# Weight preparation, skip rows, short expert turns and 21 added gathers moved in one graph and expert layer kernel

## The reference, cut to what matters

```python
xn = layernorm(x)
# 1. graph attention over 100000 edges (src, dst), 4 heads of 64
feat = (xn @ W).reshape(N, 4, 64)
ex   = exp(leaky_relu(el[src] + er[dst]) - emax[dst])
rst  = segment_sum(feat[src] * ex, dst) / segment_sum(ex, dst)
gnn  = xn + elu(rst + bias)
# 2. linear attention over all rows, 8 heads, feature map elu + 1
kv = k^T v (per head);  mix = (q kv / (q sum k)) @ wo + bo
x  = x + gnn + mix
# 3. eight experts, top two of each row
xn2 = layernorm(x);  probs = softmax(xn2 @ Wr + br);  top 2 of 8
y_e = gelu((xn2 * ln_g[e] + ln_b[e]) @ W1[e] + b1[e]) @ W2[e] + b2[e]   # 256 -> 1024 -> 256
out = x + sum over the two chosen experts of weight * y_e
```

## Time and profile before

| | |
|---|---|
| time, median of 3 runs | 1894.84 us (1893.95 to 1897.71) |
| profiled execution: its time | 1891.82 us |
| its span, first to last instruction | 1890.1 us |
| mean granted TensorE clock | 0.937 |
| PE busy | 1581.7 us (84%) |
| DVE busy | 1368.5 us (72%) |
| POOL busy | 1218.3 us (64%) |
| ACT busy | 1079.1 us (57%) |

### The profile page before, as it was taken

The page is one execution under the profiler, slowest core; times in us unless marked ns, Lnnn a source line. Parts: engine busy times, 40 slices in busy tenths (PEclk is TensorE's granted clock), DMA queues, the critical chain, the costliest instruction groups (busy, mean ns, idle before and its releaser), DMA issues. The chain is left out here.

```text
span 1890.1 us, 46784 instructions
## 1 busy us (share of the span) xinstructions
PE 1581.7 (84%) x11358; PEld 1300.0 (69%) x11358; DVE 1368.5 (72%) x3833; ACT 1079.1 (57%) x3043; POOL 1218.3 (64%) x1135
## 2 busy tenths in 40 slices
PE   7858777788787989888887778629999999999995
PEld 5635555455566777777775666517888889888884
DVE  6656567677667888888888999897666656665662
ACT  4655566566666666677666776563444444444441
POOL 2077777777777777777677776105666666666663
PEclk8978899999999999999998888658999999999998
DMA  7745565566544555555555665652333333333332
GB/s 223 247 122 138 168 174 164 165 176 179 150 117 127 155 150 150 141 152 145 142 139 179 183 202 162 200 199 45 53 48 53 49 48 50 53 50 49 46 53 24
DMA packets 149158, 239.37 MB, mean 127 GB/s; under 512 B 27536, under 2 KB 114824, under 8 KB 147624
## 3 DMA queue, kind: packets, MB, share of 16 engines
q0 software_dynamic: 61216, 132.39, 30.4%
q1 hardware_dynamic: 85944, 103.15, 16.8%
q10 hardware_dynamic: 1744, 0.85, 0.2%
HBM read 180.78 MB, written 55.52 MB: 125 GB/s over the span
## 5 line engine op out<-in xcount | busy, mean ns | idle before, releaser
L843 POOL DMA_INDIRECT w_s<-table,w_s x784 | 806.4, 1029 | 279.9 <-issue 231.4
L2092 PE MATMUL bank<-w_s 128*128 128x260 f32 x1952 | 515.9, 410 | 110.3 <-DVE w_s L1536 110.0
L2092 PEld LDWEIGHTS bank<-w_s 128*128 128x128 f32 x1952 | 378.1, 201 | 206.0 <-DVE w_s L1536 139.9
L1026 ACT ACTIVATE w_s<-w_s 128x64 f32 x976 | 260.3, 337 | 68.3 <-ACT w_s L1021 68.1
L1536 DVE SCALAR_TENSOR_TENSOR w_s<-w_s 128x256 f32<-128x256 f32 x732 | 275.7, 426 | 26.7 <-ACT w_s L1026 18.9
L2294 PE MATMUL bank<-acc,w_s 128*128 128x256 f16 (+1 forms) x2736 | 290.4, 265 | 1.6 <-DVE acc L1937 1.5
L2315 PE MATMUL bank<-w_s,acc 128*128 x2520 | 284.5, 273 | 7.2 <-DVE acc L1951 5.5
L907 POOL DMA_INDIRECT out<-mid_g,low_g x105 | 177.2, 1687 | 151.2 <-ACT mid_g L1197 90.6
L2294 PEld LDWEIGHTS bank<-acc,w_s 128*128 x2736 | 252.9, 98 | 30.7 <-issue 2.1
L2315 PEld LDWEIGHTS bank<-w_s,acc 128*128 128x128 f16 x2520 | 245.8, 98 | 37.0 <-issue 8.7
L1033 ACT COPY w_s<-bank 128x512 bf16<-128x512 bf16 x244 | 142.1, 582 | 202.8 <-PE bank L2072 202.3
(11 more groups left out here) (308 smaller groups left out, 2187.6 us busy)
## 6 DMA issues: line engine op xcount, KB each, us to landing
stage<-in_L_ffn_W SPq DMA_DIRECT2D x32, 512.0 KB, 4.2
w_s<-table,w_s POOLq DMA_INDIRECT x784
w_s<-in_x SPq DMA_DIRECT2D x48, 256.0 KB, 4.0
w_s<-xT_d SPq DMA_DIRECT2D x96, 128.0 KB
w_park<-low_g SPq DMA_DIRECT2D x18, 512.0 KB
w_s<-w_park SPq DMA_DIRECT2D x9, 1024.0 KB, 9.1
xn_d<-acc SPq DMA_DIRECT2D x7, 896.0 KB, 5.0
table<-w_s SPq DMA_DIRECT2D x24, 260.0 KB, 3.5
```

The source lines that it names most:

```text
L843: pool.indirect_dma_start(out=ring[:, u, k, :], out_offset=None, in_=table[:, :], in_offset=bass.IndirectOffsetOnAxis(ap=srcT[:, (q * RING ...
L1026: last = act.activation(m[:, e, 0:GD], rows[:, e, 0:GD], ACT.Copy, scale=m[:, e, GD:HC])
L2092: last = pe.matmul(bank[2 + k.at % 2][:, 0:ROW], hot32[:, k.at % 4, s, :], msg[:, k.at % 2, s, :], start=s == 0, stop=s == SUB - 1)
```

## The change

1. *W1 goes the way of W2.* All 16 weights are parked in 16 key turns (2 to 17), two halves in each, one through `low_g` and one through `mid_g`. The split turns are gone. SP loads each W1 from `w_park` later: experts 0 to 4 behind the late groups, 5 and 6 at the end of the walk, 7 as before. ACT now waits for a half's store of the turn before, where SP waited.
2. *Skip rows.* POOL's two additions of 128x1792 become 14 of 128x256.
3. *Fill.* POOL issues 21 small gathers (128 x 32 bytes, all of row 0 of Wr) after the skip rows, which makes its indirect DMAs 1120.
4. *Short expert turns.* The first layer of a short turn and the second layer of the turn before are mixed, eighth by eighth. `y_ready` is now waited for ahead of both, and ahead of the register load.

```diff
+LOT = 32
+FILL = -(EC + 3 * COLS) % LOT
-PARKS = 2 * (X + 1)
+PARKS = 2 * X
...
-    for n in range(SPLIT_TURNS):
-        turn(s0 + n, split, n)
...
-            def store_half(h):
-                sp.wait_ge(park_low, h + 1)
-                sp.dma_start(w_park[h // 2, :, h % 2], park_s[:, :, :]).then_inc(park_out, 16)
-                sp.wait_ge(park_out, (h + 1) * 16)
+            def store_half(e, u):
+                sp.wait_ge(park_low[u], e + 1)
+                sp.dma_start(w_park[e, :, u], park_s[u][:, :, :]).then_inc(park_out[u], 16)
...
-                if t % 2 == 0 and 0 <= h < PARKS:
-                    store_half(h)
-                    if h + 1 < PARKS:
-                        load_half(h + 1)
+                if t % 2 == 0 and 0 <= e < PARKS:
+                    for u in range(2):
+                        store_half(e, u)
+                        if e + 1 < PARKS:
+                            load_half(e + 1, u)
...
+            load_mid(0)
             for u in range(2):
-                load_w1(0, u)
-            load_mid(0)
-            group_added(0)
-            next_w1(1)
...
+                sp.wait_ge(park_out[u], 16 * PARKS)
+            sp.dma_start(b2_b, ...).then_inc(b2_in, 16)
+            sp.wait_ge(mid_out, 16 * (PAIRS + 1))
+            for g in range(5):
+                group_added(g)
+                load_w1(g)
             sp.wait_ge(msg_ready, J)
             load_mid(GROUPS - 1)
             sp.wait_ge(acc_done, J)
+            load_w1(5)
+            load_w1(6)
             load_w2(1)
...
-                pool.tensor_tensor(z, z, mid_of(g)[:, :, :], ALU.add).then_inc(x2_made, 1)
+                for k in range(RG):
+                    z = acc[:, g * RG + k, 0:D]
+                    last = pool.tensor_tensor(z, z, mid_of(g)[:, k, :], ALU.add)
+                last.then_inc(x2_made, 1)
...
+            for n in range(FILL):
+                pool.indirect_dma_start(out=filled[:, n, :], out_offset=None, in_=wr[:, :],
+                                        in_offset=bass.IndirectOffsetOnAxis(ap=fill_at[:, :], axis=0)).then_inc(filled_up, 16)
+            pool.wait_ge(filled_up, 16 * FILL)
...
-                if u == 1:
-                    act.wait_ge(park_in, (b - 1) * 16)
-                    act.activation(park_s[:, 0, :], stage[:, 0, :], ACT.Copy, scale=WSCALE).then_inc(park_high, 1)
+                if u in (1, 2):
+                    e, half = b - 2, u - 1
+                    act.wait_ge(park_in[half], (e + 1) * 16)
+                    if e:
+                        act.wait_ge(park_out[half], e * 16)
+                    act.activation(park_s[half][:, 0, :], stage[:, half, :], ACT.Copy, scale=WSCALE).then_inc(park_high[half], 1)
...
+            def dve_park(e, half):
+                dve.wait_ge(park_high[half], e + 1)
+                dve.scalar_tensor_tensor(park_s[half][:, 1, :], stage[:, half, :], WSCALE, park_s[half][:, 0, :],
+                                         ALU.mult, ALU.subtract).then_inc(park_low[half], 1)
...
+            def down_begin(s):
                 if s == 0:
                     pe.wait_ge(w2_in, X * 16)
                     pe.wait_ge(tau_turn, 1)
-                e = expert_at(pe, s)
                 if s:
                     pe.wait_ge(y_ready, s)
+                return expert_at(pe, s)
...
+            def pe_mixed(s):
+
+                e_up, e_down = up_begin(s), down_begin(s - 1)
+                for f in range(KF):
+                    up_part(s, e_up, f)
+                    down_part(s - 1, e_down, f)
...
+                if subs_of(s) == 1:
+                    pe_mixed(s)
```

More of the change, by code:

```diff
@@ L123, in past, with walk_turns @@
         return not isinstance(self.n, int) or self.n >= least
-def walk_turns(eng, slot, keys, park, queries, split, end_slot=None, late=None):
+def walk_turns(eng, slot, keys, park, queries, end_slot=None, late=None):
     def turn(b, beside, c):
@@ L145, in walk_turns @@
         turn(q0 + c, queries, c)
-    for n in range(SPLIT_TURNS):
-        turn(s0 + n, split, n)
-    for b in range(s0 + SPLIT_TURNS, end):
+    for b in range(q0 + QUERY_TURNS, end):
         turn(b, None, b)
@@ L325, in build @@
         den = acc[:, :, :].rearrange("p t (h c) -> p t h c", c=HC)[:, :, :, GD]
-        park_s = low_g[:, :, :].rearrange("p a b -> p (a b)")[:, 0:FF].bitcast(F16).rearrange("p (h f) -> p h f", h=2)
+        park_s = [whole[:, :, :].rearrange("p a b -> p (a b)")[:, 0:FF].bitcast(F16).rearrange("p (h f) -> p h f", h=2)
+                  for whole in (low_g, mid_g)]
         def w2_as(e):
@@ L474, in build @@
         consts = sem("consts")
+        fill_set, filled_up = sem("fill_set"), sem("filled_up")
         consts_v = sem("consts_v")
@@ L662, in _ @@
                 load_a(t)
-                h = t // 2 - 3
-                if t % 2 == 0 and 0 <= h < PARKS:
-                    store_half(h)
-                    if h + 1 < PARKS:
-                        load_half(h + 1)
+                e = t // 2 - 3
+                if t % 2 == 0 and 0 <= e < PARKS:
+                    for u in range(2):
+                        store_half(e, u)
+                        if e + 1 < PARKS:
+                            load_half(e + 1, u)
             def load_b(c):
@@ L2281, in pe_turn_rows, with up_begin, up_part @@
                 last.then_inc(rows_turned, 1)
-            def pe_up(s):
+            def up_begin(s):
+                pe.wait_ge(x_turn, 2 * s + 2)
+                return expert_at(pe, s)
+            def up_part(s, e, f):
                 u, rows = s % 2, rows_at(s)
-                e = expert_at(pe, s)
-                pe.wait_ge(x_turn, 2 * s + 2)
-                for f in range(KF):
-                    if f % 2 == 0 and s:
-                        pe.wait_ge(gelu_ready, 4 * s - 3 + f // 2)
-                    n = 0
-                    for k in range(KD):
-                        for wh, xh in ((0, 0), (0, 1), (1, 0)):
-                            last = pe.matmul(bank[f // 2][:, (f % 2) * FR:(f % 2) * FR + rows],
-                                             w1_s[:, bass.ds(e, 1), k, wh, f * P:(f + 1) * P].rearrange("p a b -> p (a b)"),
-                                             x_hl[:, u, xh, k, 0:rows], start=n == 0, stop=n == 5)
-                            n += 1
-                    if f % 2 == 1:
-                        last.then_inc(h_made, 1)
-            def pe_down(s):
-                u = s % 2
+                if f % 2 == 0 and s:
+                    pe.wait_ge(gelu_ready, 4 * s - 3 + f // 2)
+                n = 0
+                for k in range(KD):
+                    for wh, xh in ((0, 0), (0, 1), (1, 0)):
+                        last = pe.matmul(bank[f // 2][:, (f % 2) * FR:(f % 2) * FR + rows],
+                                         w1_s[:, bass.ds(e, 1), k, wh, f * P:(f + 1) * P].rearrange("p a b -> p (a b)"),
+                                         x_hl[:, u, xh, k, 0:rows], start=n == 0, stop=n == 5)
+                        n += 1
+                if f % 2 == 1:
+                    last.then_inc(h_made, 1)
+            def down_begin(s):
                 if s == 0:
@@ L2329, in pe_tile @@
                     pe_turn_rows(s + 1)
-                pe_up(s)
-                if s == 0:
-                    pe_unused()
-                else:
-                    pe_down(s - 1)
+                if subs_of(s) == 1:
+                    pe_mixed(s)
+                else:
+                    pe_up(s)
+                    if s == 0:
+                        pe_unused()
+                    else:
+                        pe_down(s - 1)
             pe.wait_ge(places_ready, 1)
             pe_turn_rows(0)
-            for u in range(2):
-                pe.wait_ge(low_ready[u], X - 1)
-            pe.wait_ge(w1_in, 16)
+            pe.wait_ge(w1_in, 16 * X)
             for s in range(FT):
```

105 lines of the change are left out of this document (40 added, 65 removed).

## The result

The changed kernel takes 1904.46 us (median of 19 runs, 1896.40 to 1910.45); the kernel before, beside it, 1896.07 us (19 runs). The ratio is 1.0048, 95% interval 1.0037 to 1.0058: slower by 8.4 us. The forecast was 1885.3 us and the range ended at 1897.

The account below looks back on a forecast made before the run. POOL's gathers were taken to bound the key turns, DVE the late turns; +8 +2 -18.5 -4 +3 = -9.5 us took 1894.8 to 1885.3 us, with a range of 1873 to 1897.

Parts of the forecast that it names:

- Key turns: the transfers. ... I take 2: Key turns: four 512 KB transfers in a row could delay gathers' landings; +2 us, bounds 0 and 16.
- gathers land late: Rival, 9%: in key turns the transfer row holds landings beyond 5.3 us, POOL waits every turn; 1905 us.
- The stall: Key turns: DVE's longer split instructions hold POOL's gathers; +8 us, bounds 0 and 11.5.
- the two readings there: Key turns: by the skill's rule no stall (rival, 4%, 1877 us); by a 2.53 us gather seen held, a stall.
- The form L x L / (2 x 1.32): Key turns: POOL's hold per DVE instruction of length L, gathers starting at any phase; 0.18 us for 0.684, 0.56 for 1.219.
- Late turns: Late turns: 14 DVE split instructions and a 4.1 us load wait go; -18.5 us, bounds 12 and 21 of gain.
- nothing gained in the late turns: Rival, 12%: POOL becomes the bound in the late turns, gain 12 us instead of 18.5; 1891.8 us.
- Skip rows: End of walk and second addition: DVE waits for one short POOL piece at most; -4 us, bounds -6 and 0.
- Loads at the end of the walk and fill: End of walk: 2 MB more of W1 loads, 0 us (bounds 0 and +3); 21 fill gathers in POOL's idle time, 0.
- Short turns: Experts: mixing closes a gap but waits for the previous answer; +3 us over nine turns, bounds -4 and +8.
- The DRAIN goes: Rival, 30%: filling to 35 x 32 indirect DMAs shrinks POOL's closing 7.46 us DRAIN to almost nothing; 1877.9 us.
- two remainders with one delay: Argument against the DRAIN rival: delays of 9.85 and 9.8 us after 24.5 and 34.3 lots look like a fixed cost.

Follow-up runs that it names:

- the second experiment: Two runs on the changed kernel: turns 2 to 17 with splits but only the first pair's transfers (1891.29 us), or all transfers but only the first pair's splits (1902.54 us).
- the splits alone: Changed kernel with the splits of turns 2 to 17 kept on ACT and DVE, but 30 loads and 30 stores of halves left out: 1891.29 us.
- the twins: Changed kernel with spaced single transfers, short DVE parking pieces, unmixed short turns and no fill: 1881.62 us; the same with whole skip additions: 1885.43 us.
- the repeats: Three more traces of kernels with the same key turns as the changed kernel; end of the walk and routing differ from before by -1.7 to -3.3 us.
- its own unmixed twin: Changed kernel with spaced transfers and short DVE parking pieces, the two layers of short turns one after the other: 1887.23 us, against 1894.74 us mixed.

## Why the prediction was wrong

- **The step that failed is "Key turns: the transfers. ... I take 2".** It measured 19.2 us by itself, perhaps more (the second experiment says why). The mechanism had been named, with the lag that POOL tolerates (5.3 us) and the length of a row (6 to 9 us), and the rival "gathers land late" gave its time: 1905, against 1904.46 measured, at a chance of 9%. That it came so near is partly luck: it had 22 us for the transfers, and the late turns and the experts came 3.3 us dearer than the forecast that it took over. What led astray is the ground for choosing 2 out of 0 to 16: a DMA share of 0.59, which is a mean over 313 us and says nothing of a row whose 2 MB took the plain queue some 10 us (302 to 312 us in the burst shown); and POOL's 2.4 us of waits before, which show only that a lag of 3.4 us fits under 5.3. The upper bound was too low too (16): it counted 1 us a turn.
- **The stall** (+8) was right: 8.3 us with the splits alone. Of the two readings there, the one by which this term would be 0 is wrong: VectorE's two-input instructions with nothing on GpSimd but gathers lengthened these from 1005 to 1056 ns. That reading was drawn from the Trainium skill ("SBUF — State Buffer", section "Who interferes with whom"). What the page marks as inferred there, that an instruction like `tensor_tensor` leaves descriptor generation alone, does not carry over to this pair. Its other half, that an instruction with two SBUF inputs contends with a GpSimd instruction that reads SBUF, may even cover it, since a gather takes its row numbers from an SBUF tile (the `w_s` on the right of `w_s<-table,w_s`); no run here tells whether that read is what is held. In the whole kernel the term hardly shows (1.030 against 1.018 us): the overlapping gathers hold 14.8 us there instead of 19.5. That POOL's waits take the rest away fits this, but was not tested. The form L x L / (2 x 1.32) came out for the long instruction (0.56 us said; the 32 gathers that started inside one took 0.56 us longer each), but not for what cutting it saves, half of what it said. It takes the gathers to start at any phase, and they don't: one started in 32 of 32 long instructions, and in 12 of the 32 short ones of before, where the form says 17.
- **Late turns** (-18.5): -17.2. The balance of DVE and POOL came out nearly as worked out (DVE busy 140.5 of 150 us, POOL 111.8 and 98 x 0.30 of issue, 141.2); the rival "nothing gained in the late turns" falls.
- **Skip rows** (-4): the twins say 3.8 in the medians and 2.8 in the traces; the two first traces say -3.9 for the whole stretch, the repeats -1.7 to -3.3. So the size is right within what can be told. The 0.1 us for each piece was too little: the pieces cost POOL 1.0 and 1.8 us more, and with one held by DVE 2.6 and 1.8. Whether anything waited for them was not tested.
- **Loads at the end of the walk and fill** (0 and 0): within what can be told.
- **Short turns** (+3): +5.0 between the two traces. Eight of the nine cost 0.39 us each on average (0.2 to 0.6) in the times of the answers, within the 0.2 to 0.4 that was said. The last was put at 0.8 and costs 2.05; that is the term that was mis-sized. The mechanism was right: the first matmul starts 0.79 us after the answer is read at seven of the nine (0.8 was said). A mixed turn gives its answer 1.4 to 1.9 us later (turn 7: 11.15 us after the one before instead of 9.67), and the two turns behind it take most of that back (8.15 instead of 8.52, 9.91 instead of 10.70). Behind the last one there is nothing to take it back, and the last adds wait for just this answer. Against its own unmixed twin the mixing costs more, 6.8 us in the traces and 7.5 in the medians; the unmixed code of the new kernel is 1.6 us faster than before's, and why was not isolated.
- **The DRAIN goes** (30%): wrong; 7.462 us with and without the fill. Its own counter-argument, two remainders with one delay, was the better one.

The sum by the trace is 27.7 - 17.2 - 3.9 + 5.0 = 11.6 us, where -9.5 was said; 17.2 of the 21.1 between them are the one term of the transfers. In the medians the change is 8.4 us; which term of the two traces is too large by the 3 us between cannot be told.

## What to carry to other kernels

Background transfers are to be counted by their longest row against the slack of the stream beside them, not by a mean share of the DMA engines: 2 MB in one row cost 19 us over 16 turns, and the same bytes in two rows of 1 MB some 8 (medians) to 12 us (trace) less. This rests on two layouts of one kernel. Where an engine both waits for transfers and is held by another engine, take each cause away by itself, since together they hide one another. A step that delays one result and speeds up the next ones pays only where something follows: leave the last turn out of it.

## What the runs showed of the hardware that was not expected

- In a row of four transfers the gathers' queue moved nothing for 2 us, while the plain queue moved 282 and 316 KB, though POOL had issued gathers.
- A gather that started inside DVE's two-input instruction of 128x1024 ended 0.81 to 0.94 us after it, 32 times of 32 (splits alone); beside ACT's copies alone gathers took 0.99 us.
- A seventh of POOL's addition took 0.71 to 0.73 us by itself, where 3.96 / 7 = 0.57 had been reckoned, and up to 2.50 us beside a long DVE instruction.
- POOL's first addition came 9.8 to 11.3 us after the last gather's end in the 14 traces (9.85 before). Its last wait was over 3.1 to 3.5 us after that end; in the 6.6 to 7.8 us that follow the traces show nothing that it waited for. Its closing DRAIN took 7462 ns in all 14.
